# A mixer's rows of x turned half a block earlier, with a one-column Silu ahead of x's Silu

## The reference

```
x = x + 0.5 * ffn(layernorm(x))
x = x + mixer(layernorm(x))
x = x + 0.5 * ffn(layernorm(x))

mixer(h):
  gate, xBC, dt = split(h @ in_proj_w.T)            # 1024, 1024 + 2*128, 64 heads
  x, B, C = split(silu(causal_conv4(xBC) + conv_b))
  dt = clip(softplus(dt + dt_bias), 0, 100);  A = -exp(A_log)
  per chunk of 64 tokens and head of 16 channels:
    Y_diag = ((C B^T) * exp(segment sums of A*dt)) (x*dt)   # within the chunk
    state  = sum over tokens of B * decay to the end * x*dt # carried on from chunk to chunk
    Y_off  = (C state) * exp(running sum of A*dt)
  y = (Y_diag + Y_off + D*x) * silu(gate)
  return (y * rsqrt(mean(y^2) + eps) * norm_w) @ out_proj_w.T
```

## Time and profile before

| | us |
|---|---|
| median of 3 runs | 1643.42 |
| lowest, highest | 1642.84, 1644.26 |
| the profiled execution | 1645.84 |
| its span, first to last instruction | 1644.0 |
| PE busy | 1621.2 (99%) |
| PEld busy | 1313.0 (80%) |
| DVE busy | 1034.7 (63%) |
| ACT busy | 626.3 (38%) |
| POOL busy | 378.9 (23%) |

### The profile page before, as it was taken

One profiled execution on the slowest core, in us unless ns is written; L12 is line 12 of the kernel. 1 busy time (PEld: TensorE's weight loads), 2 busy tenths in 40 slices (PEclk: granted clock), 3 DMA queues, 4 the chain that ended last, 5 costly groups with the idle time before them and its releaser, 6 DMA issues.

```text
span 1644.0 us, 25044 instructions
## 1 busy us (share of the span) xinstructions
PE 1621.2 (99%) x9672; PEld 1313.0 (80%) x9672; DVE 1034.7 (63%) x2022; ACT 626.3 (38%) x934; POOL 378.9 (23%) x298
## 2 busy tenths in 40 slices
PE   6999999999999999999999999999999999999999
PEld 3788888878888778888787888877888878888887
DVE  6543445785677877777776768777775684543333
ACT  5333343464333463333454334355333341122111
POOL 1666652012212212122122122122122121000000
PEclk9999999999999999999999999999999999999999
DMA  9745654754444444454445444445444437556763
GB/s 325 275 172 212 231 192 172 263 183 149 164 163 160 144 156 150 151 169 157 143 162 162 158 152 159 157 131 194 156 156 157 156 127 224 167 181 191 215 203 129
DMA packets 252403, 290.46 MB, mean 177 GB/s; under 512 B 14464, under 2 KB 211200, under 8 KB 243072
## 3 DMA queue, kind: packets, MB, share of 16 engines
q1 hardware_dynamic: 252288, 288.88, 53.0%
HBM read 238.51 MB, written 50.33 MB: 176 GB/s over the span
## 4 chain that ended last, share of the span: by engine, by line
PE 74%; DVE 3%; ACT 1%; issue 1%; DMA 0%; SPq 0%; ACTq 0%; DVEq 0%
PE bank L1191 31%; PE bank L1232 14%; PE bank L1147 12%; PE bank L1260 5%; PE bank L1329 3%; PE bank L1300 2%; PE bank L1316 2%; PE bank L1278 2%; PE bank L1288 1%; PE bank L1323 1%; DVE xT L1750 0%; DVE res L1776 0%; DVE m_cv L1792 0%; DVE m_L L1823 0%; DMA cum_stay<-m_aS 0%
## 5 line engine op out<-in xcount | busy, mean ns | idle before, releaser
L1191 PE MATMUL bank<-fxT,wj 128*128 128x512 f32 x1752 | 415.2, 390 | 0.0
L1191 PEld LDWEIGHTS bank<-fxT,wj 128*128 128x128 f32 x1752 | 328.7, 188 | 68.5
L1232 PE MATMUL bank<-m_wd,m_hb 128*128 128x512 f32 x1128 | 278.8, 393 | 0.0
L1232 PEld LDWEIGHTS bank<-m_wd,m_hb 128*128 128x128 f32 x1128 | 209.2, 188 | 44.9 <-issue 2.4
L1544 ACT CAST m_hb<-xn 128x512 fp32r<-128x512 f32 x96 | 59.5, 620 | 452.5 <-DVE xn L1763 452.5
L1147 PE MATMUL bank<-xT,wi 128*128 128x512 f32 x900 | 224.4, 397 | 1.6 <-DVE m_cv L1792 0.5
L1147 PEld LDWEIGHTS bank<-xT,wi 128*128 128x128 f32 x900 | 167.2, 189 | 40.1 <-issue 5.1
L1776 DVE TENSOR_TENSOR res<-bank,res 128x512 f32<-128x512 f32 x192 | 132.5, 690 | 83.0 <-PE bank L1232 80.9
L2099 POOL TENSOR_TENSOR m_L<-m_L,m_GT 128x512 f32<-128x512 f32 x36 | 52.8, 1466 | 434.4 <-ACT m_L L1553 434.4
L1763 DVE SCALAR_TENSOR_TENSOR xn<-bank,sc,xn 128x512 f32<-128x512 f32 x96 | 71.7, 747 | 121.6 <-PE bank L1191 121.5
L1538 ACT ACTIVATE xn<-bank,sc 128x512 f32<-128x512 f32 x96 | 66.1, 689 | 146.3 <-PE bank L1191 140.9
(11 more groups left out here) (224 smaller groups left out, 2317.8 us busy)
## 6 DMA issues: line engine op xcount, KB each, us to landing
wj<-ug_split SPq DMA_DIRECT2D x167, 512.0 KB, 4.2
m_wd<-dn_split SPq DMA_DIRECT2D x48, 1024.0 KB, 4.8
wi<-in_split SPq DMA_DIRECT2D x76, 512.0 KB, 3.2
ug_split<-b_wu SPq DMA_DIRECT2D x8, 2048.0 KB, 14.0
m_wo<-out_split SPq DMA_DIRECT2D x32, 512.0 KB, 4.1
wi<-ug_split SPq DMA_DIRECT2D x25, 512.0 KB, 4.2
in_split<-b_msp SPq DMA_DIRECT2D x20, 512.0 KB, 3.8
raw<-in_wug SPq DMA_DIRECT2D x8, 1024.0 KB, 6.8
```

What stands on the lines that cost most here:

```text
L1191: ins = pe.matmul(to[:], w[:, a, k, :], frm[:, b, k, :], start=(k == 0 and i == 0), stop=(k == KH - 1 and i == 2))
L1232: ins = pe.matmul(F[t % 2][:], hb[:, a, j, ck(t)], wd[:, b, j, :], start=(j == 0 and n == 0), stop=(j == 1 and n == 2))
```

## The change

`x_rows` of blocks 2 to 7 moves from the start of its block into the block before, between `from_states` and the gate's `in_proj`. On ACT `x_silu` of blocks 2 to 7 moves from behind `silu` 1 to directly behind `times`, and ahead of it comes `silu_ready`, a Silu of one column that nobody reads. Blocks 0 and 1 keep their places.

```diff
+        ready = sb("ready", [P, 1])
...
@@ PE
-                    x_rows(q, b)
+                    if b < 2:
+                        x_rows(q, b)
                     decay(q, b, 0)
...
                     ydiag(q, b)
                     from_states(q, b)
+                    if b and not end:
+                        x_rows(q, b + 1)
                     if not end:
                         in_proj(q, 6 + 2 * b)
...
@@ ACT
+            def silu_ready():
+
+                act.activation(ready[:], sc[:, 0, 0:1], ACT.Silu)
...
                     times(q, b)
+                    if b and not end:
+                        silu_ready()
+                        x_silu(q, b + 1)
                     if at:
                         hidden_high(at, 0)
...
                     if at:
                         silu(at, 1)
                     if not end:
-                        x_silu(q, b + 1)
+                        if b == 0:
+                            x_silu(q, b + 1)
                         gate(q, b + 1)
```

## The result

The changed kernel takes 1652.89 us (median of 4 runs, 1652.24 to 1655.15) against 1643.13 (4 runs): a ratio of 1.0061, interval 1.0043 to 1.0078, some 9.8 us slower. The forecast was 1648.9, slower, with a range to 1651.8: the right sign, too small a size. The profiled execution took 1655.15 us over a span of 1653.3, so 9.3 more than before's span.

A forecast was written before the change was run, and what follows sets the result against it. PE, busy 99% of the span, was taken as the bound, so its queue order and waits count. Terms: -8.8 + 0.4 + 10.3 + 4.1 - 0.5 = +5.5 us on 1643.42, giving 1648.9, range 1645.4 to 1651.8.

The forecast's parts named there:

- silu_ready and x_silu cost nothing there: Block 1 on ACT: table load and x_silu fit into free time, x_silu ending at 909.5, before from_states ends at 910.85.
- Front, -0.44 in 20 places: Starts of blocks 2 to 6: without x_rows each is 0.35 + 0.32 - 0.23 = 0.44 us shorter, -8.8 in all.
- Block 7, nothing: Start of block 7, four images: no gain counted; the second decay product hangs on ACT's Exp, so PE waits 0.44 longer.
- Second decay product, +0.02: Blocks 2 to 6: its weights wait for ACT's Exp until 2.85 instead of 2.75; 0.02 each, 20 times, +0.4 us.
- Middle, 24 x 0.43: x_rows between from_states and in_proj: four transposes take 0.43 us in each of 24 places, +10.3 in all.
- cheap rival: Rival "cheap transposes": x_rows costs 0.35 in the middle as at the front; +3.2 us, 1646.6; chance 0.20.
- the 0.45 of weight loads: Upper bound for x_rows in the middle: four transposes at a pitch of 0.11, set by loading 128 weight columns.
- The 0.41 of block 0: The nearest x_rows behind short products, in block 0 (868.42 to 868.83), used as a guide to the middle's price.
- Seven late places, 0.58 more: Block 6 of all images, block 4 of the first three: conv is late, x_rows waits; 7 x 0.58 = +4.1 us.
- The norm's wait, -0.5: Block 1, images 1 to 3: PE comes 0.43 later, so its wait for the output projection's second tile goes; -0.5 us.
- DVE's lead: Rival: DVE keeps a lead through add_down and ends conv 0.7 earlier in seven late blocks; -4.4 us, 1639.0; chance 0.07.
- The stalled decay: Rival: second decay product's wait for the first Exp adds 0.2 to 0.34 in 20 blocks; 1653 to 1656; chance 0.11.

The follow-up runs named there:

- e4: The kernel before with only ACT's half of the change (silu_ready and the early x_silu), x_rows left at its block's start: 1646.66 us, ratio 1.0013.
- e1: The kernel before plus only the unused one-column tile `ready`, allocated ahead of xc as in the change: 1647.47 us against 1644.67, ratio 1.0018.
- e2: The changed kernel with the tile `ready` allocated behind all other tiles, so those keep their places of before: 1647.96 us, ratio 1.0029 to before.
- e3: The changed kernel without silu_ready and its tile, so x_silu brings the table load itself: 1672.63 us, ratio 1.0173 to before.
- e10: e2 with the statistics of blocks 4 and 6 moved to the end of blocks 3 and 5, x_rows moved for blocks 2 to 6 only: 1640.89 us, 0.9986.

## Why the prediction was wrong, by its steps

- **What the added tile costs: the step that failed.** The prediction said "silu_ready and x_silu cost nothing there". As instructions they do (e4 against e1). It left out that silu_ready brings a tile, and that the tile moves others: 0.18% with the old order, 0.32% with the new, some 5 us of the 9.8. No term and no rival held it. By the order alone (e2, 1.0029, 4.8 us; 4.2 by periods) the forecast of 5.5 was right, in part by luck: the middle came out 1.2 us cheaper than its term and the late places 0.8 us dearer.
- **Front, -0.44 in 20 places: right.** 0.67 became 0.23.
- **Block 7, nothing: right.** 4.25 behind gate0's end against 4.26.
- **Second decay product, +0.02: right for the order.** From the end of gate0 to the product behind it, e2 has 3.20 (952.83 to 956.03), as worked out. In the changed kernel it is 3.25 (930.50 to 933.75).
- **Middle, 24 x 0.43: somewhat too much.** In e2's periods the whole move is -0.06 where nothing waits, so with -0.44 in front the middle costs some 0.38. In the changed kernel from_states, x_rows and in_proj take 4.83 (914.60 to 919.43) against some 4.44 (1.59 + 2.85), 0.39. The four transposes themselves take 0.36 (916.22 to 916.58): their starts are 0.11 apart, and in_proj starts only 0.03 behind the last. from_states ahead of them takes 1.62 instead of 1.59. So the cheap rival's 0.35 is nearly right and the 0.45 of weight loads too much. The 0.41 of block 0 misled: here too x_rows takes 0.41 where it comes late, and 0.36 where it doesn't. The prediction called itself wrong if x_rows cost under 0.38; with from_states it is at that edge. The Trainium skill's 81 ns for a product of 128 columns ("TensorE: Matmul & The Clock Gate", section "Back-to-back issue gap") gives an estimated 0.32, and 90 ns each were measured, so the measurement decides.
- **Seven late places, 0.58 more: right in place and cause, too small in size.** e2's blocks 4 and 6 are 0.70 above its others (+0.64 against -0.06). Silu started 0.11 behind conv's end instead of 0.03, and x_rows behind a wait takes 0.41 instead of 0.36. 7 x 0.70 = 4.9 instead of 4.1.
- **The norm's wait, -0.5: right.** Block 1 gains 0.22 + 0.02 (image 0's is +0.02) = 0.24, three times: -0.7.
- **Rivals.** DVE's lead did not carry: in the changed kernel scaled no longer waits for x_rows, but add_down behind it waits 2.03 for PE (rows below, image 2, block 2). The stalled decay did not come. Cheap transposes came nearly, and were paid back by the late places.

```profile
928.57 1.72 DVE L1818 TENSOR_TENSOR m_xp<-bank,m_dd 64x256 f32<-64x256 f32 x4
932.32 0.69 DVE L1788 TENSOR_TENSOR res<-bank,res 128x512 f32<-128x512 f32 x1 [2.03 <-PE bank L1233]
```

Summed over blocks 1 to 7 and the tail, e2's periods give +4.2, the changed kernel's some +9.2 (the DMA waits of blocks 0 and 7 vary and are in both). So 5.0 us are the tiles' place. Over blocks 1 to 6 alone, where those waits don't come in, it is 4.4, against 2.6 with the old order. That it costs more with the new order is measured, not explained.

## What to carry to other kernels

Where PE is busy 99% of the span, moving work earlier gives little (0.07 us a place here), and one late input costs as much as ten such places gain (0.70). Price the move in PE's own starts, and ask in every one of its places, not the typical one, whether its input is ready. A helper instruction also has a tile: allocate it last, or rerun the kernel before with the tile alone, before the order is blamed. And fix the late producer first: here moving a piece of statistics gave as much as the best order of PE.

## What the runs showed of the hardware

- **The place of tiles changes the pace of wide products, with nothing waiting.** With yh and the tiles behind it 32 or 64 bytes higher, a 128x512 product of the output projection takes 233 ns instead of 227, and 232 with 128 bytes. With the tiles from xc on 32 bytes higher, the first ten products of up0 with gate1 take 2.31 instead of 2.29, though their own operands did not move. Why wasn't found.
- **With waits of 2 us PE's clock fell in five of seven places.** In e3 each of the seven x_rows waits 2.03 to 2.05 us, behind the short products of from_states. No other run here shows a lower clock in these places. Windows of 4 us around the waits' ends (483.94, 546.79, 1022.68 and 1088.38): image 0, blocks 4 and 6, image 2, blocks 4 and 6 (us of the window, busy us of the engines, granted clock, DMA):

```profile
483.00:487.00 4.00, 3.06 (x16) 2.62 (x17) 2.54 (x5) 2.49 (x5) 1.91 (x2) 1.00 0.00 0
547.00:551.00 4.00, 4.00 (x14) 3.19 (x13) 3.61 (x7) 1.36 (x3) 2.96 (x3) 0.57 0.00 0
1022.00:1026.00 4.00, 3.32 (x10) 2.83 (x11) 2.80 (x5) 2.24 (x4) 2.16 (x2) 0.50 0.02 4
1088.00:1092.00 4.00, 3.62 (x18) 3.10 (x19) 3.10 (x5) 2.14 (x5) 2.45 (x2) 1.00 0.01 2
```

  The clock stayed at 2.4 GHz in two places and was at 1.2 GHz for most of these 4 us (0.50 to 0.58) in the other five. The blocks' periods show the price: +1.88 and +1.90 over before where the clock held, +3.34 to +3.55 in four where it fell, +4.77 in image 2's block 4, so 1.5 to 2.9 us each, 9.1 in all (3.35 + 3.50 + 3.55 + 3.34 + 4.77, less 5 x 1.89). Image 2's block 4 is the dearest because its clock stayed down longer: 0.61 over the six us from 1024, where the others have 0.79 to 0.87 in such a stretch. What tells the places apart is open. In the changed kernel the seven waits of 0.7 us left the clock at 1.00 (1072 to 1076 of its image 2).
- **One fall of the clock comes and goes between executions, worth 1.6 us.** In block 0 of image 0, PE waits 0.66 and 0.54 us around the short products of from_states, in before as in e2. Us 370 to 374 of before, then of e2:

```profile
370.00:374.00 4.00, 4.00 (x11) 3.13 (x12) 1.03 (x2) 0.50 (x1) 2.65 (x3) 0.57 0.01 2
370.00:374.00 4.00, 4.00 (x21) 3.32 (x20) 1.54 (x5) 1.73 (x3) 2.67 (x3) 1.00 0.20 53
```

  Of the 14 profiles here, 8 have this fall (before and the changed kernel among them) and 6 don't, and in these that block's period is 1.6 us shorter (15.4 against 17.0 in before). So e1's profiled span (1643.9) is no longer than before's (1644.0), though e1 is the slower kernel. The table above leaves block 0 out and is free of this.
- **A small DVE instruction beside POOL lasted until POOL's had ended.** Before, the first step of the statistics, of 4 columns, takes 1.26 us from 1054.29. POOL works from 1053.99:

```profile
1054.29 1.26 DVE L162 TENSOR_TENSOR m_mv<-m_st 128x4 f32<-128x4 f32 x1
```

```profile
1053.99 1.54 POOL L2099 TENSOR_TENSOR m_L<-m_L,m_GT 128x512 f32<-128x512 f32 x1 [17.40 <-ACT m_L L1553]
```

  It ends at 1055.55, POOL's instruction at 1055.53, and so it is in all seven places (1.25 to 1.26 us each). In e10, where it was moved to a time without POOL, it takes 0.15:

```profile
981.63 0.15 DVE L162 TENSOR_TENSOR m_mv<-m_st 128x4 f32<-128x4 f32 x1
```

  These 1.1 us are a large part of conv's lateness in the seven places. An estimate from the earlier trace rows: without them conv of image 2's block 6 would end at 1064.6 instead of 1065.71, early enough for x_rows behind from_states at 1065.57. That was not run by itself.
